# Eight chunks shared out anew: decay forms, router and norm forms, TensorE's order in chunk 1, and 72 increments ahead of VectorE's loop

## The chip, the core and the metric

One NeuronCore of a Trainium2 chip runs the whole program. The metric is its device time in microseconds, the median of three runs. All arithmetic that counts is float32.

## What is computed

The input is x, 8 sequences of 1024 tokens with 256 features. Four blocks follow one another, each with a normalization ahead of it and a residual sum behind it:

```python
x = x + scan_block(layernorm(x))      # selective scan, 512 channels x 16 states
x = x + ffn(layernorm(x))             # 16 experts, top 6, softmax gates
x = x + attention(layernorm(x))       # flow attention, linear in the tokens
x = x + ffn(layernorm(x))             # the same experts again
```

The scan block is what matters here:

```python
x_in, z = split(layernorm(x) @ in_proj)          # 256 -> 2 x 512
x_conv  = silu(conv4(x_in))
Bm, Cm  = split(x_conv @ x_proj)                 # 16 + 16
delta   = clip(softplus(x_conv @ dt_proj), 1e-4, 10)
h = exp(clip(delta * A, -10, 0)) * h + delta * Bm * x_conv   # token by token
h = h * min(1, 10 / |h|)                         # at every 16th token only
y = sum(Cm * h) + D * x_conv
out = layernorm(x + (y * silu(z)) @ out_proj)
```

The norm of h over its 16 states is looked at after every 16th token, so a scan runs over 16 tokens and no more before it must be bounded.

## The kernel before

**Tiles and chunks.** The 8192 tokens are 64 tiles of 128 tokens. Channels lie on partitions (4 blocks of 128), so a tile has 4 x 16 = 64 rows of states for each partition. A tile is worked through in eight chunks (c = 0 to 7) of 16 tokens. In each chunk GpSimd writes the inputs u * B into the state buffer (`inputs`, L394), ScalarE writes the decays into PSUM (`exponentials`, L456), VectorE runs one scan over 64 x 17 elements (`scan`, L1022), ScalarE squares the last states (`squares`, L462), VectorE sums them (`reduce`, L1030), ScalarE makes the factor (`norms`, L468 and L473), and VectorE bounds the states for the next chunk (`bound`, L1040 and L1043). GpSimd multiplies the states by C (`product`, L363), and TensorE transposes and sums these products in four quarters (`sum_states`, L730).

**Stages in step i.** Each engine has its own instruction list and an order written out by hand in its `step(i, k, stages)`; semaphores alone tie the engines together. Around the scan of tile i, a step also does the front of the tiles behind it (normalization of tile i + 4, projection and convolution of tile i + 3, gate and delta of tile i + 2), the back of tile i - 1 and i (return of the sums by `copy_sums` and `sums_back`, gating L1185, output projection L831, second norm L1194 to L1224, residual sum L414), the router of tile i - 2 (`route_norm`, `route`, `logits`, `route_scores`, `route_step`, `route_gate`), and the experts of tile i - 3 (`experts_mm` L764 on TensorE, one pair of experts a chunk; `expert_sums` L1106 on VectorE, two forms a chunk).

**Decay forms.** Ahead of the exponentials, ScalarE makes relu(10 + delta * A) for all 128 tokens of a tile, one activation for each of the 64 rows (`decays`, L447). They are those of tile i + 1, made during step i. `DECAYS` gives the first row of each chunk: chunks 0 to 7 make 6, 7, 6, 11, 7, 13, 14 and 0 of them. The first of a tile waits until delta is there, and the last releases the next tile's exponentials.

**VectorE's chunk.** `start(c)` is the scan and the two expert sums, `halfway(c)` the sum of squares, `end(c)` the bound; the forms of the other stages are placed between them. `route_step` has eight small steps for the choice of six experts; `router(lo, hi)` issues some of them. In chunk 3 both last norm forms (L1221, L1224) are made. `route_gate` makes the selection (L1096) and the gates (L1098) in chunk 7. GpSimd's `extra` makes u in chunk 1, sz (silu of z) in chunk 4, the gated xcv in chunk 5 and the residual sum in chunk 7.

**TensorE in chunk 1.** First the return of the sums (`sums_back`, L738, which waits for ScalarE's copy yT, L479), then the transposes of the router's input (`route`, L746), then the input projection (L823, which waits for xnT, L574).

**Loops.** `pipeline` unrolls the first and the last tiles. Between them every engine runs a loop of its own in which one turn is two tiles: on VectorE 28 turns from tile 4 on, on ScalarE 27 from tile 6 on. VectorE's increments at its start (`head_start`) and `settle` are instructions that only add to a semaphore.

After the 64 tiles the second stage (`merged`, some 1570 us) does attention and the second experts; in it VectorE calls `route_gate` once a tile.

## Time and profile before

| | us |
|---|---|
| median of 3 runs | 4571.68 |
| lowest, highest | 4569.64, 4571.75 |
| the profiled execution | 4568.96 |
| its span, first to last instruction | 4567.2 |
| TensorE busy | 4017.2 |
| VectorE busy | 3473.9 |
| ScalarE busy | 3079.6 |
| GpSimd busy | 2647.6 |

The profile is one execution on the chip. Engines are PE (TensorE, with PEld for its weight loads), DVE (VectorE), ACT (ScalarE), POOL (GpSimd) and SP (the queue that issues the transfers). A timeline row gives the start, the duration, the engine, the line of the kernel, what is written and read, a count where several are merged, and in brackets how long the engine was idle before it and what released it. The releaser is inferred; where the engine named had long been done, the cause is another one. Busy sums count overlaps of one instruction's end with the next one's start twice, so a full engine can seem slightly more than full.

### The profile page before, as it was taken

The page shows a single profiled execution, that of the slowest core. Times are in us where ns is not written, and L with a number is a line of the kernel's source. Part 1 is how long each engine was busy: PE and PEld are TensorE (multiplying, and loading weights), DVE is VectorE, ACT ScalarE, POOL GpSimd, SP SyncE. Part 2 cuts the span into 40 slices and gives each one's busy share as a digit, 9 for nine tenths or more (in the row PEclk, how much of TensorE's full clock was granted, in tenths as well). Part 3 has the DMA queues.
Part 4 walks back from the last instruction along what each step waited for, and adds up shares of the span by engine and source line. Part 5 has one row for each costly group of instructions (what it writes and reads, how often), then busy time and mean ns, then how long its engine had stood idle before and what let it go on. Part 6 is the DMA issues. An engine that isn't in the chain of part 4 may idle for free. (4 is left out here: it accounts for less than half of the span.)

```text
span 4567.2 us, 72130 instructions
## 1 busy us (share of the span) xinstructions
PE 4017.2 (88%) x19008; PEld 2604.4 (57%) x19008; DVE 3473.9 (76%) x7970; ACT 3079.6 (67%) x9040; POOL 2647.6 (58%) x1412
## 2 busy tenths in 40 slices
PE   6788888888888888888888888877999999999999
PEld 5666666566665666656666566643454454454454
DVE  4788888888888888888888888884566666676576
ACT  6888888888888888888888888863333333323321
POOL 5988988888888898888888888880000000000000
PEclk8999999999999999999999999999999999999999
DMA  3111111111111111111111111110000000000000
GB/s 112 52 58 52 59 49 49 57 53 55 51 49 57 49 62 49 49 57 49 56 55 49 57 49 51 59 48 15 23 16 8 16 16 6 16 17 6 6 8 10
DMA packets 91401, 188.71 MB, mean 41 GB/s; under 512 B 15872, under 2 KB 57600, under 8 KB 90624
## 3 DMA queue, kind: packets, MB, share of 16 engines
q1 hardware_dynamic: 91136, 186.11, 12.5%
q14 instruction: 213, 1.74, 0.1%
q8 instruction: 52, 0.85, 0.1%
HBM read 168.24 MB, written 17.83 MB: 41 GB/s over the span
## 5 line engine op out<-in xcount | busy, mean ns | idle before, releaser
L764 PE MATMUL ps<-w_x,mxT 128*128 128x512 f32 x4096 | 1994.7, 616 | 172.9 <-DVE macc L1106 171.5
L1106 DVE SCALAR_TENSOR_TENSOR macc<-ps,gate,macc 128x256 f32<-128x256 f32 x2048 | 981.0, 479 | 556.1 <-PE ps L764 458.5
L1022 DVE TENSOR_TENSOR_SCAN hb<-ps_dA,hb 128x1088 f32<-128x1088 f32 x512 | 1240.5, 2423 | 138.7 <-POOL hb L394 68.9
L394 POOL TENSOR_TENSOR hb<-u,bbc 128x1024 f32<-128x1024 f32 x512 | 1202.5, 2349 | 246.5 <-DVE hb L1040 199.5
L363 POOL TENSOR_TENSOR prod<-hb,cbc 128x1024 f32<-128x1024 f32 (+2 forms) x640 | 1190.0, 1864 | 136.0 <-DVE hb L1022 94.5
L764 PEld LDWEIGHTS ps<-w_x,mxT 128*128 128x128 f32 x4096 | 739.8, 195 | 894.3 <-issue 606.2
L447 ACT ACTIVATE zr<-dt,aneg 128x128 f32<-128x128 f32 x4096 | 1240.1, 388 | 0.0
L456 ACT ACTIVATE ps_dA<-zr 128x1024 f32<-128x1024 f32 x512 | 518.5, 1013 | 0.0
L730 PE MATMUL ps<-ident,prod 128*128 128x128 f32 x4096 | 493.8, 274 | 14.1 <-POOL prod L363 14.1
L730 PEld LDWEIGHTS ps<-ident,prod 128*128 128x128 f32 x4096 | 459.5, 142 | 19.7 <-POOL prod L363 17.6
L462 ACT ACTIVATE sq<-hb 128x64 f32<-128x64 f32 x512 | 158.1, 309 | 295.5 <-DVE hb L1022 292.1
L509 ACT ACTIVATE ex<-lgt,ms 128x16 f32<-128x16 f32 x128 | 39.2, 306 | 356.7 <-DVE ms L1063 356.5
L847 PEld LDWEIGHTS ps<-xin,dcw 128*128 128x128 f32 x2048 | 240.9, 193 | 21.3 <-issue 19.5
L877 PEld LDWEIGHTS ps<-xcv,w_dt 128*128 128x128 f32 x2048 | 245.3, 196 | 2.0
L877 PE MATMUL ps<-xcv,w_dt 128*128 128x128 f32 x2048 | 244.3, 279 | 0.0
L847 PE MATMUL ps<-xin,dcw 128*128 128x128 f32 x2048 | 240.9, 276 | 0.0
L823 PE MATMUL ps<-xnT,w_in 128*128 128x128 f32 x1024 | 185.4, 358 | 4.9 <-ACT xnT L574 3.5
L823 PEld LDWEIGHTS ps<-xnT,w_in 128*128 128x128 f32 x1024 | 179.5, 272 | 5.8 <-ACT xnT L574 4.0
L1040 DVE SCALAR_TENSOR_TENSOR hb<-ps_dA,hb 128x64 f32<-128x64 f32 x480 | 127.8, 266 | 67.9 <-ACT ps_dA L473 66.8
L738 PE MATMUL ps<-ident,yT 128*128 128x128 f32 x256 | 59.6, 320 | 135.4 <-ACT yT L479 135.4
L1030 DVE TENSOR_REDUCE nrs<-sq 128x4 f32<-128x64 f32 x512 | 110.2, 215 | 88.5 <-ACT sq L462 85.0
L738 PEld LDWEIGHTS ps<-ident,yT 128*128 128x128 f32 x256 | 33.5, 155 | 239.1 <-ACT yT L479 205.8
(200 smaller groups left out, 4850.5 us busy)
## 6 DMA issues: line engine op xcount, KB each, us to landing
bbc<-bcd SPq DMA_DIRECT2D x128, 512.0 KB, 3.7
cbc<-bcd SPq DMA_DIRECT2D x128, 512.0 KB, 3.7
xt<-in_x SPq DMA_DIRECT2D x128, 128.0 KB, 3.3
x2d<-macc SPq DMA_DIRECT2D x64, 128.0 KB, 1.7
out_dram<-macc SPq DMA_DIRECT2D x64, 128.0 KB, 1.7
w_x<-in_w_x SPq DMA_DIRECT2D x1, 4096.0 KB, 15.5
hb<-x2d SPq DMA_DIRECT2D x32, 128.0 KB, 2.3
sz<-x2d SPq DMA_DIRECT2D x16, 128.0 KB, 2.2
```

Of the source, the lines that this page charges most:

```text
L363: return TT(dst, states, cc, ALU.mult)
L394: TT(hb[c % 2][:].rearrange("p (e n) s -> p e n s", e=EB)[:, :, :, 1:SL], u[k][:, :, t0:t0 + CH].rearrange("p e (n s) -> p e n s", n=1).br ...
L447: last = act(zr[k][:, s, :], dt[:, s // N, :], ACT.Relu, bias=10.0, scale=aneg[:, s:s + 1])
L456: act(dA3[:, :, 1:SL], zr[k][:, :, c * CH:(c + 1) * CH], ACT.Exp, bias=-10.0).then_inc(M["dA"], 1)
L462: act(sq[:], hb[c % 2][:, :, CH:SL].rearrange("p a b -> p (a b)"), ACT.Square).then_inc(M["sq"], 1)
L730: last = mm(YT[:, h * P:(h + 1) * P], prod[:, n, h % 2 * QT:(h % 2 + 1) * QT, :].rearrange("p t e -> p (t e)"), ident[:], start=(h % 2 == ...
L764: last = mm(banks[p % len(banks)][:], mxT[k][:, j, :], w_x[:, j, p * 512:(p + 1) * 512], start=(j == 0), stop=(j == KD - 1))
L823: last = mm(F0[:, m * P:(m + 1) * P], w_in[:, j, m * P:(m + 1) * P], xnT[:, j, :], start=(j == 0), stop=(j == KD - 1))
L847: last = mm(F0[:, e * P:(e + 1) * P], dcw[:, e * TAPS + t, :], xin[:, e, t:t + P], start=False, stop=(e == EB - 1 and t == TAPS - 1))
L877: last = mm(F0[:, m * P:(m + 1) * P], w_dt[:, e, m * P:(m + 1) * P], xcv[k][:, e, :], start=False, stop=(m == EB - 1 and e == EB - 1))
L1022: V.tensor_tensor_scan(states, dA, states, 0.0, ALU.mult, ALU.add).then_inc(M["scan"], 1)
L1106: STT(macc[k][:], banks[(e // 2) % len(banks)][:, (e % 2) * D:(e % 2 + 1) * D], gate[k][:, e:e + 1], macc[k][:], ALU.mult, ALU.add).then_i ...
```

## The change

The decay forms per chunk become 5, 10, 5, 11, 6, 11, 11 for chunks 0 to 6, and the first 5 of the following tile are made in chunk 7, behind the delta that they need. GpSimd makes sz in chunk 3 instead of 4. TensorE does the input projection first in chunk 1, then the router's transposes, then the return of the sums. On VectorE the last norm form goes from chunk 3 to 4; the router's steps 2 and 3 go from chunk 5 to 4, steps 4 and 5 from chunk 6 to 5, and steps 6 and 7 stay in chunk 6, the first of them now ahead of the sum of squares' place; the selection becomes a helper of its own, `route_selection`, and goes from chunk 7 to 6 (in the second stage it stays where it was). Ahead of VectorE's loop stand 72 more increments of the settle semaphore. `DECAYS` now has eight entries: the chunk's first row for chunks 0 to 6, and the total. No instruction is added to or taken from a tile.

```diff
@@ -22,7 +22,7 @@
 X, TOPK = 16, 6
 ROUTER = 11
 DT_TOP, DT_BOTTOM = math.log(math.expm1(10.0)), math.log(math.expm1(1e-4))
-DECAYS = (0, 6, 13, 19, 30, 37, 50, 64, 64)
+DECAYS = (5, 10, 20, 25, 36, 42, 53, 64)
 
 
 AHEAD = 64
@@ -401,7 +401,7 @@
                     g.wait_ge(M["ldt"], AHEAD + i + 2)
                     g.wait_ge(M["xcv"], AHEAD + i + 2)
                     TT(u[1 - k][:], dt[:], xcv[1 - k][:], ALU.mult).then_inc(M["u"], 1)
-                if c == 4 and "G" in stages:
+                if c == 3 and "G" in stages:
                     g.wait_ge(M["ss"], AHEAD + i + 2)
                     g.wait_ge(M["yg"], AHEAD + (i if "B" in stages else 0))
                     TT(sz[1 - k][:], zt[:], sg[:], ALU.mult).then_inc(M["sz"], 1)
@@ -613,8 +613,10 @@
                             act(dt[:], dtt[:], ACT.Ln, bias=1.0).then_inc(M["ldt"], 1)
                         if X_ and in_time(i, X // 2 - 1):
                             route_init(i - 2, k, x1b[k][:], lambda: a.wait_ge(R["o"][k], AHEAD + (i - 2 - k) * 8))
-                    if G_ and DECAYS[c] < DECAYS[c + 1]:
+                    if G_ and c < NC - 1:
                         decays(i + 1, 1 - k, DECAYS[c], DECAYS[c + 1])
+                    if F and c == NC - 1:
+                        decays(i + 2, k, 0, DECAYS[0])
                     if c == 0 and B:
                         copy_sums(i - 1, 1)
                     if c == 5 and S_:
@@ -809,11 +811,6 @@
                     if c == 0 and B:
                         sum_states(i - 1, 3)
                     if c == 1:
-                        if B:
-                            sums_back(i - 1, 1)
-                        if X_:
-                            pe.wait_ge(M["bcv"], AHEAD + min_tiles(i + 2, stages))
-                            route(i - 2, k, F1)
                         if isinstance(i, int) and i == -2:
                             pe.wait_ge(s_win, 16)
                         if F:
@@ -823,6 +820,11 @@
                                     last = mm(F0[:, m * P:(m + 1) * P], w_in[:, j, m * P:(m + 1) * P],
                                               xnT[:, j, :], start=(j == 0), stop=(j == KD - 1))
                             last.then_inc(M["xi"], 1)
+                        if X_:
+                            pe.wait_ge(M["bcv"], AHEAD + min_tiles(i + 2, stages))
+                            route(i - 2, k, F1)
+                        if B:
+                            sums_back(i - 1, 1)
                     if c == 2:
                         if B:
                             pe.wait_ge(M["yg"], AHEAD + i)
@@ -1090,10 +1092,13 @@
                     v.wait_ge(R["router"], AHEAD + n * ROUTER + 8)
                     TS(ms[:, 12:13], ms[:, 5:6], ms[:, 8:9], 1e-10, ALU.mult, ALU.mult).then_inc(R["router"], 1)
 
-            def route_gate(n, k):
+            def route_selection(n):
 
                 v.wait_ge(R["router"], AHEAD + n * ROUTER + 5)
                 TT(selp[:], ex[:, 0:X], rest[:, 0:X], ALU.subtract).then_inc(R["router"], 1)
+
+            def route_gate(n, k):
+
                 v.wait_ge(R["router"], AHEAD + n * ROUTER + 10)
                 TS(gate[k][:], selp[:], ms[:, 9:10], None, ALU.mult).then_inc(R["router"], 1)
 
@@ -1219,14 +1224,15 @@
                     V.reciprocal(sc[:, 12:13], sc[:, 11:12]).then_inc(M["r3"], 1)
                     v.wait_ge(M["r3"], AHEAD + i)
                     STT(oo[:], oo[:], mv[:, 2, 0:1], ga_row[:], ALU.subtract, ALU.mult).then_inc(M["o3"], 1)
+                end(3)
+
+                start(4)
+                router(0, 2)
+                halfway(4)
                 if B:
                     v.wait_ge(M["o3"], AHEAD + i)
                     STT(oo[:], oo[:], sc[:, 12:13], be_row[:], ALU.mult, ALU.add).then_inc(M["o4"], 1)
-                end(3)
-
-                start(4)
-                router(0, 2)
-                halfway(4)
+                router(2, 4)
                 if G_:
                     v.wait_ge(M["r1"], AHEAD + i + 2)
                     V.tensor_copy(r1b[1 - k][:], r1a[1 - k][:]).then_inc(M["keep"], 1)
@@ -1236,9 +1242,9 @@
                 end(4)
 
                 start(5)
-                router(2, 3)
+                router(4, 5)
                 halfway(5)
-                router(3, 4)
+                router(5, 6)
                 if F:
                     v.wait_ge(M["z"], AHEAD + i + 3)
                     v.wait_ge(M["sz"], AHEAD + (i + 2 if G_ else 0))
@@ -1249,18 +1255,19 @@
                 end(5)
 
                 start(6)
-                router(4, 5)
                 if L_:
                     v.wait_ge(M["st1"], AHEAD + i + 4)
                     settle()
                     V.bn_aggr(mv[:, 0, :], st[:, 0, :]).then_inc(M["mv1"], 1)
-                router(5, 6)
+                router(6, 7)
                 if L_:
                     v.wait_ge(M["mv1"], AHEAD + i + 4)
                     TS(sc[:, 0:1], mv[:, 0, 1:2], 1e-5, None, ALU.add).then_inc(M["vp"], 1)
                     TS(sc[:, 1:2], mv[:, 0, 1:2], D / (D - 1.0), 1e-30, ALU.mult, ALU.max).then_inc(M["vp"], 1)
                 halfway(6)
-                router(6, 8)
+                router(7, 8)
+                if X_:
+                    route_selection(i - 2)
                 end(6)
                 if L_:
                     v.wait_ge(M["qs"], AHEAD + i + 4)
@@ -1301,6 +1308,8 @@
             TT(left[96:P, :], left[96:P, :], rows_of_split[96:P, :], ALU.subtract).then_inc(s_split, 1)
             v.wait_ge(s_split, 4)
             V.tensor_copy(rows_of_split[96:P, :], left[96:P, :]).then_inc(s_zero, 1)
+            for _ in range(72):
+                settle()
             v.wait_ge(s_zero, 4)
             pipeline(v, step)
 
@@ -1420,6 +1429,7 @@
                         for q in range(4 * (p - 6), 4 * (p - 5)):
                             route_step(r + NTILES, q)
                     if p == 7:
+                        route_selection(r + NTILES)
                         route_gate(r + NTILES, r % 2)
                 if b < NB and not early:
                     attend(b, s)
```

## Rows read from the trace of the kernel before

**Rows 1.** Page, part 1: busy us (share) and instructions of each engine

```profile
PE 4017.2 (88%) x19008; PEld 2604.4 (57%) x19008; DVE 3473.9 (76%) x7970; ACT 3079.6 (67%) x9040; POOL 2647.6 (58%) x1412
```

**Rows 2.** Stretches: length, busy of PE, PEld, DVE, ACT, POOL, clock, DMA

```profile
190.68:2993.24 2802.56, 2393.64 (x13690) 1744.97 (x13688) 2354.01 (x4715) 2399.55 (x7256) 2440.90 (x1298) 0.95 0.16 53
```

**Rows 3.** Waits of VectorE, 190.68 to 2993.24: total us, times, longest

```profile
DVE hb L1022 <- POOL hb L394: 68.9, 21, 3.6
DVE macc L1106 <- PE ps L764: 67.9, 53, 2.0
DVE nrs L1030 <- ACT sq L462: 65.6, 176, 0.5
DVE hb L1040 <- ACT ps_dA L473: 54.8, 117, 0.7
DVE oo L1194 <- PE ps L831: 39.8, 59, 0.7
DVE hb L1022 <- issue: 18.6, 6, 3.1
```

**Rows 4.** Timeline of VectorE at a jump: start, us, line, operands [idle before]

```profile
1566.45 0.26 DVE L1043 SCALAR_TENSOR_TENSOR hb<-ps_dA,hb 128x64 f32<-128x64 f32 x1
1570.32 2.42 DVE L1022 TENSOR_TENSOR_SCAN hb<-ps_dA,hb 128x1088 f32<-128x1088 f32 x1 [3.61 <-POOL hb L394]
```

**Rows 5.** DMA queue 14: 1570.32:1663.14, then 1 us from 1568, 1571, 1584, 1616, 1651

```profile
q14 instruction: 5, 0.04, 0.2%
q14 instruction: 1, 0.01, 1.9%
q14 instruction: 1, 0.01, 2.0%
q14 instruction: 1, 0.01, 6.0%
q14 instruction: 1, 0.01, 5.2%
q14 instruction: 1, 0.01, 2.1%
```

**Rows 6.** Timeline of ScalarE at its jump

```profile
1566.70 0.49 ACT L505 ACTIVATE macc<-x1b,ms 128x256 f32<-128x256 f32 x1
1567.10 0.58 ACT L552 ACTIVATE xn<-xt,sc 128x256 f32<-128x256 f32 x1
```

**Rows 7.** Timeline of VectorE at the start

```profile
6.01 0.06 DVE L996 MEMSET c_eps<- 128x1 f32 x1 [6.01 <-issue]
```

**Rows 8.** Timeline of TensorE in tile 31, and at 1579

```profile
1521.56 0.44 PE L807 MATMUL ps<-ident,xn 128*128 128x128 f32 x2 [1.11 <-ACT xn L552]
1523.76 1.98 PE L764 MATMUL ps<-w_x,mxT 128*128 128x512 f32 x4
1528.37 0.44 PE L738 MATMUL ps<-ident,yT 128*128 128x128 f32 x2 [2.62 <-ACT yT L479]
1529.15 2.97 PE L823 MATMUL ps<-xnT,w_in 128*128 128x128 f32 x16
...
1579.13 1.95 PE L823 MATMUL ps<-xnT,w_in 128*128 128x128 f32 x16
```

**Rows 9.** Timeline of ScalarE, the projection's operand

```profile
1525.51 0.79 ACT L574 ACTIVATE xnT<-ps,be_in,ga_in 128x128 f32<-128x128 f32 x2
```

**Rows 10.** Stretch with the granted clock (0.50)

```profile
1530.00:1532.00 2.00, 2.00 (x11) 2.00 (x11) 1.64 (x3) 1.97 (x9) 2.00 (x3) 0.50 0.00 0
```

**Rows 11.** Timeline of ScalarE, decay forms and the square behind xn

```profile
1507.75 3.89 ACT L447 ACTIVATE zr<-dt,aneg 128x128 f32<-128x128 f32 x13
...
1522.84 0.31 ACT L462 ACTIVATE sq<-hb 128x64 f32<-128x64 f32 x1 [1.33 <-DVE hb L1022]
```

**Rows 12.** Timeline of VectorE, the bound of chunk 6

```profile
1513.39 0.27 DVE L1040 SCALAR_TENSOR_TENSOR hb<-ps_dA,hb 128x64 f32<-128x64 f32 x1 [0.71 <-ACT ps_dA L473]
```

**Rows 13.** Timeline of GpSimd, chunk 3

```profile
1544.20 2.35 POOL L394 TENSOR_TENSOR hb<-u,bbc 128x1024 f32<-128x1024 f32 x1 [1.29 <-DVE hb L1040]
```

6 lines of the change are left out of this document (3 added, 3 removed).

## Prediction

> **What bounds the kernel now.** I read the page first. VectorE, ScalarE, GpSimd and TensorE are all close to full until about 3000 us, then only TensorE is [rows 1]. The change touches the first stage (the scan over 64 tiles of 128 tokens); of the second it only splits one VectorE helper in two without moving an instruction, so I leave it alone. In the middle of the first stage, from the first scan of tile 3 to that of tile 62, 59 tiles take 2802.56 us, 47.5 us a tile [rows 2]. Divided by 59, the busy sums are 41.4 us for GpSimd, 40.7 for ScalarE, 40.6 for TensorE and 39.9 for VectorE: nothing is saturated, the tile is 6 us longer than its fullest engine. Where those microseconds are stands in VectorE's waits, since VectorE carries the serial chain (scan, square sum, bound, next scan) [rows 3]. The reader should see two kinds there.
>
> First, 27 waits before a scan, 68.9 + 18.6 = 87.5 us, 3.2 us each. They are one per turn of the loop (28 turns of two tiles, 27 jumps back). The one at 1570.32 starts when the last instruction of the turn, of 1566.45, is done, and nothing that it could wait for is late [rows 4]: the profile names a GpSimd instruction only because that is the last one before it.
>
> Second, waits for other engines inside the tile: 67.9 (expert sums for TensorE) + 65.6 (square sums for ScalarE) + 54.8 (bound for ScalarE) + 39.8 (residual for the output projection) = 228.1 us, 3.87 us a tile. Without both kinds a tile is (2802.56 - 87.5 - 228.1) / 59 = 42.15 us; that is VectorE's own work with its gaps.
>
> **Part 1: 72 increments ahead of VectorE's loop.** What are the 3.2 us? In the turn that starts at 1570, five packets of instructions are fetched, 0.04 MB, so 8 KB or 128 instructions of 64 bytes each [rows 5]. One lands in the gap itself, one right behind it, then one at 1584, 1616 and 1651. I counted in the instruction lists that the kernel builds to: VectorE has 526 instructions ahead of the loop and 339 in it, ScalarE 986 and 321. At 1584 VectorE stands at about number 50 of the loop, at 1616 (just in the second tile) at 176, at 1651 at 305: 128 apart. So blocks of 128 begin at numbers 50, 178 and 306, the loop lies in four of them, and with the next one fetched ahead the first has been dropped when the loop jumps back. ScalarE's loop of 321 shows what happens when it fits: at its jump, between the instruction at 1566.70 and the one at 1567.10, there is no gap [rows 6], and the five packets are all VectorE's. Three blocks and the one fetched ahead stay; that is my reading of two loops, an inference. If number 50 starts a block, the loop starts 78 into one; 72 more instructions move that to 150 - 128 = 22, and 22 + 339 = 361 is under 384: three blocks. ScalarE gets about 5 more instructions ahead of its loop; its absence of fetches says that it starts at most 63 into a block. So all 27 stalls go: **-87.5 us**. Bounds: 0 (the size of the store is not what I infer) and -87.5. I take the end, since a loop that fits is there to see.
>
> The Trainium skill, page "Runtime: NRT & Kernel Launch", section "Instruction fetch mechanics", speaks against this: it has 32 KiB of instructions in blocks of 16 KiB, only two lines, and a taken branch to a target outside that window stalls. By that rule 339 instructions never stay at any place, and this term would be 0. Packets of 8 KB and ScalarE's loop without a gap [rows 5, 6] disagree with it.
>
> The price of the increments is paid once, at 17 us, where VectorE goes straight from its set-up to the first instruction of the pipeline, on which the first convolution waits. VectorE's first 56 increments lie in the 6.01 us ahead of its first instruction [rows 7], so one costs at most 0.11 us: 72 cost 0 to 7.7. I take **+4**, since that row has the start of the program in it as well.
>
> **Part 2: TensorE's order in chunk 1.** Now TensorE holds at the return of the sums for ScalarE's copy of yT, 2.62 us at 1528.37, and the input projection behind it starts only at 1529.15, although its operand was done at 1526.30 [rows 9]. It then runs at half speed: 2.97 us against 1.95 in the next tile [rows 8], with a granted clock of 0.50, so 1.2 GHz [rows 10], after an idle of 2.6 us. The expert product behind it is late, and VectorE waits for it 53 times, 1.3 us each [rows 3]. With the projection first, TensorE works through that idle; the product and the output projection end some 2 us earlier. The waits of 67.9 and 39.8 go. What is late next: the sums return behind projection and transposes. The pair of 1523.76 is done at 1525.7; with part 3 that is 1527.2, plus 1.95 is 1529.15, plus some 0.6 for the two small steps is 1529.75, against 1528.8 now. VectorE's gating waits for it: about 0.4 us a tile is given back, part of it hidden by a wait of 0.2 that chunk 1 has now.
>
> **Part 3: decay forms.** 64 a tile as before, 0.30 us each (13 in 3.89 us) [rows 11]. Chunks 0 to 6 had 6, 7, 6, 11, 7, 13, 14 and get 5, 10, 5, 11, 6, 11, 11; chunk 7 had none and gets 5. ScalarE's sum is the same. The forms go away where ScalarE is late: the 176 waits for a square are three in a tile, 0.37 us each, in chunks 1, 5 and 7 [rows 3], and behind the 13 forms of chunk 5 the bound of chunk 6 waits 0.71 [rows 12]. With 2 and 3 forms fewer in chunks 5 and 6, 0.6 and 0.9 us, those go; chunk 0's loss of one takes 0.3 off the wait in chunk 1. What the five in chunk 7 cost: the normalized input xn of the next tile comes 1.5 us later. Now ScalarE has 1.33 us free behind it [rows 11], so the next square is late by about 0.2, in the shadow of two expert sums and the norm forms. TensorE stands idle for xn some 0.7 us longer than now (1.11 us [rows 8]), since the pair ahead of it ends later too in a tile without the other waits, and runs from there without a break.
>
> **Part 4: VectorE's forms and sz.** The last norm form goes from chunk 3 to 4, where two router forms join it; the selection goes from chunk 7 to 6. Chunks 4 and 6 grow, chunks 3, 5 and 7 shrink by as much together. Net 0: the count is the same, these chunks are VectorE's own either way, and what waits for them is off the path (the residual sum is in chunk 7; the convolution's result is needed by ScalarE only when its forms are done). GpSimd's sz goes from chunk 4 to 3, where GpSimd now waits 1.29 us for VectorE [rows 13], about the length of sz, and what follows in chunk 4 moves up by as much.
>
> **Sum.** Of 228.1 us of waits I leave 0.9 us a tile: 0.4 from part 2 and 0.5 for four engines that are then 93 to 96% full and meet with little to spare. That is 53 us left, **-175 us**; a tile is 43.05. Bounds: nothing left, -228, and half left, -114. Profiled execution: 4568.96 - 87.5 - 175 + 4 = 4310.5; its time is 2.7 below the median, so **4313 us**. With the bounds: 4260 to 4378.
>
> **The rivals.**
> (a) The clock falls elsewhere. TensorE idles nearly 2 us ahead of xn; idles of 1.3 us are not followed by a fall now, one of 2.6 is. If it falls there, the transposes, an expert pair and the projection (6 us of work) take up to 3 us more, and half of it comes back to VectorE through the returned sums: 1 to 1.5 us a tile, 59 to 89 us: 4372 to 4402. For it: that is exactly where the forms put the gap. Against: behind it TensorE is busy for 12 us on end. 16%.
> (b) The jump still costs 3.2 us, because the first block is dropped wherever the loop lies (or ScalarE's loop now loses its own): 4313 + 87 = 4400. For it: no loop of VectorE is to be seen without the gap. Against: [rows 5, 6]. 12%. This is the case that the rule of the Trainium skill, quoted above, gives.
> (c) Everything fits and nothing of the waits is left but 0.3 us a tile: 4270 to 4285. 10%.
> (d) Slower: the clock does not come back. If TensorE stays at 1.2 GHz for most of a tile, its 40.6 us of work grow: 12 us of full-speed work at half speed make 53, longer than the 47.5 of now, and TensorE bounds the tile; from 7 us on the gain is gone. For 59 tiles 5 us more is +300: about 4870. Against: granted clock is 0.95 over the stretch [rows 2], and every fall now ends within 4 us. 3%.
> (e) The moves gain only what they cost (an engine that is nearly full takes over) and the jump stays: within 0.2% of now. 2%.
>
> **How the numbers follow.** Forecast 57%, with its own range 4285 to 4360. The range must reach to (a) and (b): 4265 to 4402. A difference under 0.2% (9 us) can't be told from none here. Faster: forecast, (a), (b), (c) = 95%; same 2%, slower 3%.
>
> **What would show it.** No gap of 3 us before a scan, and no instruction packets in the middle of the stage: part 1 right. Input projection at 1.95 us in every tile and no wait of the expert sums in chunk 2: part 2. No wait of the bound in chunk 6: part 3. A granted clock under 1 in the first 10 us of a tile: (a). A tile above 44 us with no such stretch would mean that my shares of waits were not where the next limit is, which would make the prediction wrong.

## The result and the profile after

The changed kernel takes 4430.3 us (median of 4 runs, 4425.88 to 4433.15) against 4571.7 for the kernel before in the same session: a ratio of 0.9687, 95% interval 0.9671 to 0.9704. That is 141 us faster, and 117 us slower than the 4313 predicted, above the top of the range (4402). Its profiled execution has a span of 4427.8 us.

The table shows where the 139.4 us between the two spans lie (us, each stretch up to the next), counted from the first scan of tile 0, of tile 3 and of tile 62:

| stretch | before | after | difference | predicted |
|---|---|---|---|---|
| to the first scan | 62.20 | 70.05 | +7.85 | +4 |
| tiles 0 to 2 | 128.48 | 126.97 | -1.5 | 0 |
| tiles 3 to 61 | 2802.56 | 2656.93 | -145.6 | -262.5 |
| the rest | 1573.96 | 1573.85 | -0.1 | 0 |

All but some 2 us of the miss are in the middle of the first stage: 116.9 us. The busy sums of this stretch stand in the following row of the after kernel's stretches, to be read beside [rows 2] (columns: length, busy PE, PEld, DVE, ACT, POOL, granted clock, DMA share, GB/s). A tile takes 2656.93 / 59 = 45.03 us.

```profile
197.02:2853.95 2656.93, 2308.05 (x13692) 1702.80 (x13690) 2496.47 (x4715) 2391.34 (x7254) 2446.97 (x1299) 0.99 0.17 56
```

The reader should look at the third busy sum. VectorE has the same 4715 instructions as in [rows 2] and is busy for 142.5 us more. This sum is the stretch less the engine's idle time, so overlaps do not count twice in it, other than the text on the profile above has it; added up one by one, the durations of its instructions grew from 2531 to 2733 us. ScalarE and GpSimd are within 9 us of their sums there, and TensorE has 86 us less, its clock having risen from 0.95 to 0.99. The waits come first. These are VectorE's in the after kernel, same stretch (total us, times, longest), beside [rows 3]:

```profile
DVE sg L1190 <- PE ps L740: 36.3, 58, 1.2
DVE macc L1111 <- PE ps L766: 12.8, 12, 1.2
...
DVE nrs L1032 <- ACT sq L462: 3.7, 23, 0.2
```

No wait before a scan is left. Of the four kinds of 228.1 us, 16.5 are left (12.8 + 3.7), and a new kind has come, the gating's wait for the returned sums, 36.3. Together that is 52.8 us, 0.90 us a tile, just the sum that the prediction left standing. That it fits so well is partly luck: the gating has 0.6 where 0.4 was said, the others 0.3 where 0.5 was said. Still, the waits went as forecast. What went wrong is the rest of the tile: (2656.93 - 52.8) / 59 = 44.14 us, where the prediction had 42.15.

The groups of VectorE's instructions show where (a form is one instruction of an engine). Mean ns of one stands behind the busy sum. First four groups of the kernel before, from 200 to 2800 us, then the same four of after:

```profile
L1221 DVE SCALAR_TENSOR_TENSOR oo<-oo,mv,ga_row 128x256 f32<-128x256 f32 x55 | 26.7, 485 | 2.0
L1224 DVE SCALAR_TENSOR_TENSOR oo<-oo,sc,be_row 128x256 f32<-128x256 f32 x55 | 26.7, 485 | 2.0
L1096 DVE TENSOR_TENSOR selp<-ex,rest 128x16 f32<-128x16 f32 x54 | 31.6, 584 | 0.0
L1098 DVE TENSOR_SCALAR gate<-selp,ms 128x16 f32<-128x16 f32 x54 | 35.3, 654 | 1.9
```

```profile
L1226 DVE SCALAR_TENSOR_TENSOR oo<-oo,mv,ga_row 128x256 f32<-128x256 f32 x58 | 68.6, 1183 | 2.1
L1234 DVE SCALAR_TENSOR_TENSOR oo<-oo,sc,be_row 128x256 f32<-128x256 f32 x58 | 120.9, 2085 | 0.0
L1098 DVE TENSOR_TENSOR selp<-ex,rest 128x16 f32<-128x16 f32 x57 | 100.8, 1768 | 0.0
L1103 DVE TENSOR_SCALAR gate<-selp,ms 128x16 f32<-128x16 f32 x57 | 47.6, 836 | 0.0
```

The same instructions on the same operands: the last norm form takes 2085 ns instead of 485, the selection 1768 instead of 584, the first norm form 1183 instead of 485. Together the four have 5.87 us a tile instead of 2.21: 3.66 us, 216 us over the 59 tiles. No other group of VectorE changed by more than 3.0 us in the stretch, and those that changed by over 0.8 became shorter, some 14 us in all. The timeline of the after kernel, GpSimd and VectorE side by side, says what they wait for inside:

```profile
1432.27 2.24 POOL L363 TENSOR_TENSOR prod<-hb,cbc 128x1024 f32<-128x1024 f32 x1
1433.80 0.98 DVE L1226 SCALAR_TENSOR_TENSOR oo<-oo,mv,ga_row 128x256 f32<-128x256 f32 x1
1434.47 1.46 POOL L407 TENSOR_TENSOR sz<-zt,sg 128x512 f32<-128x512 f32 x1
...
1438.17 2.50 POOL L363 TENSOR_TENSOR prod<-hb,cbc 128x64 f32<-128x64 f32 x2
1438.77 2.18 DVE L1234 SCALAR_TENSOR_TENSOR oo<-oo,sc,be_row 128x256 f32<-128x256 f32 x1
...
1450.35 2.27 POOL L363 TENSOR_TENSOR prod<-hb,cbc 128x1024 f32<-128x1024 f32 x1
1450.87 1.78 DVE L1098 TENSOR_TENSOR selp<-ex,rest 128x16 f32<-128x16 f32 x1
```

Each form starts under a GpSimd product and ends when it does: the last norm form at 1440.95, the product at 1440.67; the selection at 1452.65, the product at 1452.62. The first norm form starts at 1433.80, the product ends at 1434.51, and the form ends 0.27 us behind it. It is so in all 59 tiles of the stretch: each of the four forms starts under a GpSimd instruction and ends just behind it, the norm forms by 0.26 to 0.28 us (but for two of the first, which end behind the next one), the selection and the gate by 0.02 to 0.04. The selection and the gate already were held so in all 59 tiles of the kernel before, for a shorter remainder. There, the two norm forms ran in the hole of 1.29 us that [rows 13] shows on GpSimd:

```profile
1540.66 2.25 POOL L363 TENSOR_TENSOR prod<-hb,cbc 128x1024 f32<-128x1024 f32 x1
1542.85 0.48 DVE L1221 SCALAR_TENSOR_TENSOR oo<-oo,mv,ga_row 128x256 f32<-128x256 f32 x1
1543.37 0.48 DVE L1224 SCALAR_TENSOR_TENSOR oo<-oo,sc,be_row 128x256 f32<-128x256 f32 x1
```

The product ends at 1542.91 and the next GpSimd instruction starts at 1544.20; but for the first 0.06 us both forms lie between. The four long groups have their inputs and their output in SBUF. Forms of VectorE that read PSUM (xin, zt, the gating) kept their 0.68 to 0.69 us, xin at 1433.01 under the first of these products.

**What the theory is, and its rival.** Theory: those four forms are held by GpSimd's instructions, which costs the 2 us a tile that the prediction lacks. Rival: the held time costs nothing by itself, since VectorE would wait anyway, and the missing 2 us come from TensorE, whose idle time ahead of the normalized input grew from the 1.11 us of [rows 8] to 2.4 to 2.5, with the clock falling behind it in some tiles. For the theory speaks that 47 of the 59 tiles show no fall of the clock and still take 44.7 us.

### The profile page after: what moved, and what is told of

It is laid out like the page before. It is cut to its first block, busy times and chain, and to the rows that moved or that the text cites. A ratio compares the mean times of both kernels' runs of the same rounds, so it can differ in the third digit from the quotient of the medians.

```text
span 4427.8 us, 72202 instructions
## 1 busy us (share of the span) xinstructions
PE 3935.4 (89%) x19008; PEld 2565.6 (58%) x19008; DVE 3621.2 (82%) x7970; ACT 3072.6 (69%) x9040; POOL 2654.1 (60%) x1412
## 4 chain that ended last, share of the span: by engine, by line
PE 49%; issue 22%; DVE 15%; POOL 5%; ACT 4%; DVEq 1%; ACTq 0%; POOLq 0%
PE ps L766 27%; DVE macc L1111 6%; PE ps L879 5%; POOL prod L363 3%; PE ps L914 3%; PE ps L732 2%; PE ps L820 2%; PE ps L896 2%; ACT zr L447 2%; POOL xcv L410 2%; PE ps L872 1%; PE ps_dA L914 1%; DVE xin L1221 1%; DVE sg L1286 1%; DVE xcv L1241 1%
## 5 line engine op out<-in xcount | busy, mean ns | idle before, releaser
L766 PE MATMUL ps<-w_x,mxT 128*128 128x512 f32 x4096 | 1967.9, 609 | 202.1 <-DVE macc L1111 202.1
L766 PEld LDWEIGHTS ps<-w_x,mxT 128*128 128x128 f32 x4096 | 730.0, 192 | 932.5 <-issue 599.4
L363 POOL TENSOR_TENSOR prod<-hb,cbc 128x1024 f32<-128x1024 f32 (+2 forms) x640 | 1191.2, 1866 | 53.0 <-DVE hb L1024 44.8
L732 PE MATMUL ps<-ident,prod 128*128 128x128 f32 x4096 | 507.7, 279 | 14.6 <-POOL prod L363 14.6
L809 PE MATMUL ps<-ident,xn 128*128 128x128 f32 x128 | 28.7, 307 | 166.5 <-ACT xn L552 164.2
L820 PEld LDWEIGHTS ps<-xnT,w_in 128*128 128x128 f32 x1024 | 128.8, 198 | 34.0 <-issue 16.6
L809 PEld LDWEIGHTS ps<-ident,xn 128*128 128x128 f32 x128 | 13.1, 143 | 216.0 <-ACT xn L552 110.2
L861 PEld LDWEIGHTS ps<-xnT,w_in 128*128 128x128 f32 x1024 | 124.4, 192 | 21.3 <-issue 19.5
L914 PE MATMUL ps<-zr,prod 128*128 128x512 f32 x288 | 134.4, 592 | 0.0
L820 PE MATMUL ps<-xnT,w_in 128*128 128x128 f32 x1024 | 130.1, 282 | 4.1 <-ACT xnT L574 4.1
```

The costliest lines, as they stand in the source:

```text
L363: return TT(dst, states, cc, ALU.mult)
L732: last = mm(YT[:, h * P:(h + 1) * P], prod[:, n, h % 2 * QT:(h % 2 + 1) * QT, :].rearrange("p t e -> p (t e)"), ident[:], start=(h % 2 == ...
L766: last = mm(banks[p % len(banks)][:], mxT[k][:, j, :], w_x[:, j, p * 512:(p + 1) * 512], start=(j == 0), stop=(j == KD - 1))
L820: last = mm(F0[:, m * P:(m + 1) * P], w_in[:, j, m * P:(m + 1) * P], xnT[:, j, :], start=(j == 0), stop=(j == KD - 1))
L914: last = mm(QUAD[s % 4][:], w_a[:, w, kk, j * P:(j + 1) * P], xTa[:, kk, g * TG:(g + 1) * TG], start=(kk == 0), stop=(kk == KD - 1))
```

## The experiments

All ratios are against runs of the kernel before on the same chip; after is 4430.3 us. Those with one run only have no ratio. The runs belong to five sessions, in which the kernel before had medians of 4563.9 to 4573.4 us, so a difference from after of 15 us or less isn't clear of noise by the times alone; where it matters, the middle stretch of the profiled executions stands beside it (after: 2656.93 us).

### 1. The increments alone, and the change without them

Kernel before with nothing but the 72 increments:

```diff
             v.tensor_copy(rows_of_split[96:P, :], left[96:P, :]).then_inc(s_zero, 1)
+            for _ in range(72):
+                settle()
             v.wait_ge(s_zero, 4)
```

> The kernel before with nothing but the 72 increments ahead of VectorE's loop. Theory (the loop fits into three blocks of 128 instructions and is kept): the 27 waits of 87.5 us go, the start costs the 6.3 us seen in the changed kernel, so about 4490, with 79 instruction packets instead of 213 and in-tile waits as before (3.9 us a tile). Rival (the gap is hidden in the changed kernel by something else that changed, place decides nothing): 213 packets, the 27 gaps stay, about 4578.

Measured: 4476.8 us, ratio 0.9795 (0.9776 to 0.9814). The waits of 87.5 us are gone and the others are as they were in [rows 3], 3.83 us a tile; the tile went from 47.50 to 45.91, and the first scan moved from 62.20 to 68.67. Instruction packets, from the page's DMA part: 213 in the kernel before, here

```profile
q14 instruction: 78, 0.64, 0.0%
```

The other way round, the changed kernel without the increments:

> The changed kernel without the 72 increments; all moved forms stay. Theory: the gap of 3.2 us is back at each of 27 jumps and the start is 6.3 us shorter: 4430 + 87.5 - 6.3 = 4511, 213 packets. Rival (the gap came from the old order of the forms): no gap, about 4424.

Measured: 4514.9 us, ratio 0.9876 (0.9856 to 0.9896), 214 packets, and the gap is back at each jump:

```profile
1547.72 2.42 DVE L1024 TENSOR_TENSOR_SCAN hb<-ps_dA,hb 128x1088 f32<-128x1088 f32 x1 [3.31 <-POOL hb L394]
```

And the changed kernel with 100 increments in place of 72, so that the loop starts 50 into a block of 128 (22 + 28) and 50 + 339 = 389 is over 384:

> The changed kernel with 100 increments ahead of VectorE's loop instead of 72. Theory (blocks of 128, four kept, the loop starts 78 + 100 - 128 = 50 into one and 50 + 339 = 389 is over 384): the loop lies in four blocks again, the 27 gaps and some 213 packets are back: 4430 + 87.5 + 2.5 = 4520. Rival (any shift that moves the loop far enough is good): no gap, 79 packets, 4433.

Measured: 4569.4 us (one run), 213 packets, and in the stretch from 200 to 2800 us:

```profile
DVE hb L1024 <- POOL hb L394: 74.6, 21, 4.1
...
DVE hb L1024 <- issue: 14.8, 5, 3.2
```

The gap is back at 26 jumps, all that lie in that stretch. So it isn't the presence of increments, but where the loop begins: by the prediction's count starts of 22, 50 and 78 into a block were tried, and only 22, with the loop in three blocks, is without the gap. The total is 49 us above what was expected. A further 0.33 us stands ahead of xin once a turn (8.9 in all), where the profile names nothing that it waits for, and 27 of 59 tiles have the long chunk 1 described in 6, against 12 in after.

### 2. Three forms back in their old places

The changed kernel with the last norm form in chunk 3, the selection in chunk 7 and sz in chunk 4:

```diff
-                if c == 3 and "G" in stages:
+                if c == 4 and "G" in stages:
...
                     STT(oo[:], oo[:], mv[:, 2, 0:1], ga_row[:], ALU.subtract, ALU.mult).then_inc(M["o3"], 1)
+                if B:
+                    v.wait_ge(M["o3"], AHEAD + i)
+                    STT(oo[:], oo[:], sc[:, 12:13], be_row[:], ALU.mult, ALU.add).then_inc(M["o4"], 1)
...
-                if X_:
-                    route_selection(i - 2)
...
                 if X_:
+                    route_selection(i - 2)
                     route_gate(i - 2, k)
```

> The changed kernel with three moves undone: the last norm form back in chunk 3, sz back in chunk 4, the selection back in chunk 7. Theory (VectorE's forms that take both operands from SBUF are held while a GpSimd form runs, and the three moves put them into GpSimd's busy times): last norm form from 2.09 to about 0.49 us, the one before it from 1.17 to 0.49, selection from 1.77 to 0.59, together 3.5 us a tile less VectorE time; part of it comes back as waits, so a tile of 42 to 43.3 instead of 45.03 and 4250 to 4330 in all. Rival (the tile is held by another engine, and VectorE's longer forms only fill the time): the forms are short again but waits take their place, tile 44.5 to 45, 4410 to 4430.

Measured: 4388.6 us, ratio 0.9605 (0.9587 to 0.9623): 42 us faster than after, and above the range expected. The forms are short again, the selection at 909 ns and the last norm form, by its group (200 to 2800 us), at 485:

```profile
L1229 DVE SCALAR_TENSOR_TENSOR oo<-oo,sc,be_row 128x256 f32<-128x256 f32 x59 | 28.6, 485 | 2.1
```

But the waits are not those of after. From 200 to 2800 us of this kernel:

```profile
DVE macc L1111 <- PE ps L766: 43.3, 81, 0.7
DVE sg L1190 <- PE ps L740: 42.9, 58, 1.2
DVE hb L1042 <- ACT ps_dA L473: 37.9, 58, 0.7
DVE nrs L1032 <- ACT sq L462: 14.0, 84, 0.2
```

138 us now stand there where after has 52.5. The tile without its waits is 41.96 us, the floor of the prediction (42.15) or a little less. So the theory holds for the floor, and the rival is right on the larger part of the sum: the tile without its waits lost 2.18 us against after, and the waits took 1.48 of it back. Not all of that comes from the short forms. In chunk 7, sz in chunk 4 delays ScalarE's silu of xcv by 0.41 us, and the expert product behind it is late by 0.66, some 40 us in all. With the selection back and sz left in chunk 3 (experiment 4) VectorE waits only 12.5 us for it there, so some 27 us are the price of moving sz. In chunk 6, without the selection, VectorE arrives at the bound 0.66 us before ScalarE's factor.

### 3. One operand from PSUM

To see whether it is the operand and nothing else, the last norm form stays in chunk 4 and reads its second operand from a PSUM bank, which holds the convolution's result, in place of the bias row in SBUF. It leaves out the norm's bias in all tiles but the last ones.

```diff
-                    STT(oo[:], oo[:], sc[:, 12:13], be_row[:], ALU.mult, ALU.add).then_inc(M["o4"], 1)
+                    if F:
+                        v.wait_ge(M["conv"], AHEAD + i + 3)
+                        STT(oo[:], oo[:], sc[:, 12:13], F0[:, 0:D], ALU.mult, ALU.add).then_inc(M["o4"], 1)
+                    else:
+                        STT(oo[:], oo[:], sc[:, 12:13], be_row[:], ALU.mult, ALU.add).then_inc(M["o4"], 1)
```

> The changed kernel, with the last norm form at the same place in chunk 4 but its second operand read from a PSUM bank (the convolution's, free at that time) instead of the bias row in SBUF. That leaves out the addition of the norm's bias row in all tiles but the last ones. Theory (two operands in SBUF are what is held): the form takes about 0.49 us instead of 2.09, all else as before it, and the tile loses up to 1.6 us. Rival (the form is held by its place, for example its input or its output is awaited): still about 2.1 us.

Measured (one run): 4391.1 us. The group and the timeline of this kernel:

```profile
L1236 DVE SCALAR_TENSOR_TENSOR oo<-oo,sc,ps 128x256 f32<-128x256 f32 x59 | 27.8, 471 | 0.0
```

```profile
1419.37 2.49 POOL L363 TENSOR_TENSOR prod<-hb,cbc 128x64 f32<-128x64 f32 x2 [0.20 <-DVE hb L1024]
1420.45 0.47 DVE L1236 SCALAR_TENSOR_TENSOR oo<-oo,sc,ps 128x256 f32<-128x256 f32 x1
```

Same place, same size, same product beside it: 471 ns instead of 2085, and in all 59 tiles it ends 0.79 us or more before the product does. That is the holding, shown. Of the 1.61 us of this form, 95 us over 59 tiles, 39 reached the time; the neighbours took some (first norm form 1362 instead of 1183, selection 1899 instead of 1768), and waits for TensorE rose from 49.1 to 89.0 (52.6 for the gating, 36.4 for the experts). The 36 waits for the experts stand in chunk 1, and just as many tiles of this kernel have the long chunk 1 of experiment 6.

### 4. One form at a time

The selection alone back in chunk 7:

> The changed kernel with the selection back in chunk 7, next to the gates. Theory (held by GpSimd's product in chunk 6): 1.77 us becomes 0.6 to 0.9, chunk 6 shrinks by 1.1 at most and chunk 7 grows by 0.6, so 0.3 to 0.6 us a tile, 4395 to 4412. Rival: the wait for the bound's factor in chunk 6 takes its place in full, 4430.

Measured: 4415.2 us, ratio 0.9666 (0.9643 to 0.9689), 15 us less than after and just outside what was expected; the two ratios' intervals overlap, but the middle stretch is 12.9 us shorter as well (2644.05). The selection takes 917 ns, the gate 655: 1.03 us less a tile held, with the first norm form 1.18 in all. 20.5 us of it came back as the bound's wait for ScalarE's factor in chunk 6.

The last norm form alone back in chunk 3, sz staying there too:

> The changed kernel with the last norm form back in chunk 3, sz staying there too. Theory: GpSimd is busy there now, with the product and then sz, so the form is held until sz is done, 1.2 to 1.7 us instead of 2.09: chunk 4 loses 2.1, chunk 3 gains 1.2 to 1.7; a gain of 0.4 to 0.9 us a tile, 4380 to 4408. Rival (the form is short wherever the convolution's neighbourhood is left): 0.49 us, 4340.

Measured: 4388.9 us, ratio 0.961 (0.9587 to 0.9632), as expected. It takes 1258 ns here, not 485, since sz now fills the hole of [rows 13]. This kernel is as fast as that of experiment 2, although its four forms have 5.15 us a tile and those have 2.82: how long the forms are held does not by itself tell the time.

Both together, with the increments moved out of the start into VectorE's part of step -2:

> The changed kernel with the last norm form back in chunk 3 and the selection back in chunk 7, sz still in chunk 3, and the increments inside VectorE's first step. Theory: the gains of the two runs before add up (41 and 15 us against the changed kernel's 4430), and the start's 6.3 us come on top: 4360 to 4375. Rival: they overlap, 4385.

Measured: 4383.9 us, ratio 0.9601 (0.9585 to 0.9618): only 5 us better than the norm form alone, where the first scan alone comes 6.8 us earlier (63.94 against 70.76). The gains of the two forms don't add. From 200 to 2800 us of this kernel, the bound's wait for ScalarE's factor is back with 26.4 us, and the gating's wait is 43.6 where after has 36.0.

### 5. TensorE's order back

The changed kernel with the old order in chunk 1 (return of the sums, router's transposes, projection):

> The changed kernel with TensorE's old order in chunk 1 (return of the sums, transposes, then the input projection). Theory (the new order is what ends VectorE's wait in chunk 2): chunk 2 grows by the 1.5 to 2 us that it lost, chunk 1 gives back about 0.5, so 1 to 1.5 us a tile, 4490 to 4520. Rival (the decay forms alone would have done it): within 15 us of 4430.

Measured: 4436.5 us, ratio 0.9714 (0.9698 to 0.973). The rival named there was right and the expectation wrong by 54 us: the new order is worth 6 us, both in the times and in the middle stretch (2662.89), and the ratios' intervals just overlap. Waits from 200 to 2800 us:

```profile
DVE macc L1111 <- PE ps L766: 32.4, 31, 1.2
DVE oo L1199 <- PE ps L833: 25.0, 57, 0.8
```

The waits for the output projection (39.8 in [rows 3]) and for the experts (67.9) are there as the old order makes them, but smaller, a bound's wait of 6.2 stands beside them, and the gating's 36.3 is gone. The sum is 1.13 us a tile against 0.90: the new order exchanges one set of waits for another.

### 6. TensorE's idle time ahead of the normalized input, and the clock

In after, 12 of the 59 tiles take about 46.3 us instead of 44.7, with 6.6 to 6.9 us in chunk 1 where the others have 5.1 to 5.2. TensorE's timeline at the start of such a tile, and then of a normal one:

```profile
1505.94 0.43 PE L809 MATMUL ps<-ident,xn 128*128 128x128 f32 x2 [2.50 <-ACT xn L552]
1506.21 2.89 PE L732 MATMUL ps<-ident,prod 128*128 128x128 f32 x16
1508.90 2.62 PE L766 MATMUL ps<-w_x,mxT 128*128 128x512 f32 x4
```

```profile
1461.15 0.44 PE L809 MATMUL ps<-ident,xn 128*128 128x128 f32 x2 [2.42 <-ACT xn L552]
1461.42 1.91 PE L732 MATMUL ps<-ident,prod 128*128 128x128 f32 x16
1463.17 1.88 PE L766 MATMUL ps<-w_x,mxT 128*128 128x512 f32 x4
```

After an idle of 2.50 us the transposes take 2.89 instead of 1.91 us and an expert pair 2.62 instead of 1.88. The granted clock stands in the last column but two, first for 2 us of the slow tile and then for 8 us of the normal one:

```profile
1508.00:1510.00 2.00, 2.00 (x8) 1.48 (x7) 1.87 (x2) 1.91 (x8) 1.78 (x2) 0.50 0.03 7
1461.00:1469.00 8.00, 7.85 (x48) 5.85 (x49) 6.84 (x15) 7.56 (x26) 7.78 (x5) 1.00 0.28 79
```

0.50 is 1.2 GHz, 1.00 is 2.4 GHz. To take the idle time away, the five forms in chunk 7 go:

```diff
-DECAYS = (5, 10, 20, 25, 36, 42, 53, 64)
+DECAYS = (0, 5, 15, 23, 34, 42, 53, 64)
...
-                    if F and c == NC - 1:
-                        decays(i + 2, k, 0, DECAYS[0])
```

> The changed kernel with no decay forms in chunk 7: chunks 0 to 6 make 5, 10, 8, 11, 8, 11, 11. Theory (the five forms hold back xn by 1.5 us, TensorE idles 2.4 us ahead of it, the clock falls in about one tile of five and the sums' return is 0.5 us late in the others): idle back to 1.1 us or less, no tile of 46.3, the wait of the gating for the sums gone, so 0.5 us off most tiles and 1.9 off eleven, 4380 to 4400. Rival (ScalarE is full and the forms cost as much in chunks 2 and 4): 4430 or more.

Measured: 4415.8 us, ratio 0.9673 (0.965 to 0.9697). TensorE's idle ahead of xn fell from 140.0 to 57.8 us between 200 and 2800 us (1.0 us a tile), no tile has the long chunk 1, and the granted clock is 1.00 over the whole middle: the clock part is as expected. The gain is 15 us, not 30 or more, and the ratios' intervals overlap; the middle is 12.2 us shorter (2644.76). Two waits stand, 200 to 2800 us:

```profile
DVE nrs L1030 <- ACT sq L462: 37.0, 86, 0.6
DVE sg L1188 <- PE ps L738: 27.9, 57, 0.5
```

The forms that left chunk 7 delay the square of chunk 3 (32.9 us), and the return of the sums still stands behind projection and transposes.

### 7. The forms together, and the best kernel

All four forms back to back at the end of chunk 6, increments in step -2, `DECAYS` (5, 10, 20, 25, 34, 40, 50, 64):

> The changed kernel with all four forms that GpSimd holds (both norm forms, selection, gates) one behind another at the end of chunk 6, the 72 increments inside VectorE's first step where it waits for TensorE anyway (two times 36), and decay forms 5, 10, 5, 9, 6, 10, 14, 5. Theory (a form is held until the running GpSimd form ends; behind it the next ones slip in while VectorE has the port): one hold a tile instead of four, so the four forms take 2.5 to 3 us together instead of 5.87; start 6 us shorter; a tile of 42.8 to 43.8 and 4290 to 4355 in all. Rival (each form is held anew, since GpSimd takes its turn between two): some 5 us again, 4400 to 4430.

Measured: 4379.9 us, ratio 0.9592 (0.9576 to 0.9608), above the range expected. Of the 50 us that it gains on after, 7.6 lie ahead of the first scan, since the increments now stand where VectorE waits anyway; the middle gains 41, as much as in experiment 2. Two tiles of this kernel:

```profile
1422.96 0.47 DVE L1269 SCALAR_TENSOR_TENSOR oo<-oo,mv,ga_row 128x256 f32<-128x256 f32 x1
1423.07 2.58 POOL L363 TENSOR_TENSOR prod<-hb,cbc 128x1024 f32<-128x1024 f32 x1
1423.35 0.17 DVE L1098 TENSOR_TENSOR selp<-ex,rest 128x16 f32<-128x16 f32 x1
1423.47 2.45 DVE L1274 SCALAR_TENSOR_TENSOR oo<-oo,sc,be_row 128x256 f32<-128x256 f32 x1
1425.84 0.22 DVE L1103 TENSOR_SCALAR gate<-selp,ms 128x16 f32<-128x16 f32 x1
...
1465.98 1.24 DVE L1269 SCALAR_TENSOR_TENSOR oo<-oo,mv,ga_row 128x256 f32<-128x256 f32 x1
1466.87 2.46 POOL L363 TENSOR_TENSOR prod<-hb,cbc 128x1024 f32<-128x1024 f32 x1
1467.14 2.22 DVE L1098 TENSOR_TENSOR selp<-ex,rest 128x16 f32<-128x16 f32 x1
1469.28 0.47 DVE L1274 SCALAR_TENSOR_TENSOR oo<-oo,sc,be_row 128x256 f32<-128x256 f32 x1
```

Free, the four take 0.47, 0.17, 0.47 and 0.22 us. In a group, not all of them pay: in 36 of the 59 tiles one is held and the others pass, in 23 two are, the first norm form and the selection. In the second tile shown, the first norm form ends at 1467.22, behind the GpSimd instruction ahead of the product, which ends at 1466.93, and the selection at 1469.36, behind the product, which ends at 1469.33. Which ones they are changes from tile to tile. The four have 3.69 us a tile instead of 5.87. But 36 of 59 tiles now have the long chunk 1 with the clock fall, and the waits are 2.06 us a tile. The last experiment takes that away as in 6:

```diff
-DECAYS = (5, 10, 20, 25, 34, 40, 50, 64)
+DECAYS = (0, 5, 15, 23, 32, 40, 50, 64)
```

> The same kernel as the grouped one (the four norm and router forms together at the end of chunk 6, the increments inside VectorE's turn, 4379.9 us), with one thing changed: no decay form in chunk 7; the 64 are 5, 10, 8, 9, 8, 10, 14 in chunks 0 to 6. In the grouped kernel 59.4 us of waits stand ahead of the expert sums and 56.0 ahead of the gating, and both were in the tiles whose clock is low in the first 10 us. Theory (the clock falls because TensorE stands idle some 2.5 us for the normalized input, which chunk 7's forms hold back): no tile with chunk 1 over 6 us, expert-sum waits down from 59.4 to 10 to 20, gating waits from 56 to about 30, TensorE's products back from 291 to 270 to 277 ns; against that 0.6 us in every second tile for a square, some 18 us: 4325 to 4350 us. Rival (the sums' return and the square take the gain, as in the kernel without the five forms that kept its own place for the norm forms, where only 15 us were left): 4360 to 4375. Rival 2 (the clock falls anyhow): 4380 or more.

Measured: 4356.8 us (4352.78 to 4357.07), ratio 0.9544 (0.9528 to 0.956), between the two ranges given, 3 us from the rival's. No tile has a long chunk 1 (only tile 3 still has the clock fall, behind an idle of 2.1 us), the transposes of the products are at 273 ns a piece against 291, and no wait of VectorE for the experts is left. What came instead is the square, more than the 18 us allowed for it:

```profile
DVE nrs L1032 <- ACT sq L462: 50.0, 145, 0.6
DVE sg L1190 <- PE ps L740: 27.8, 57, 0.5
```

The clock fall is not gone altogether. In 11 of the 59 tiles it now comes in chunk 6, behind an idle of 1.9 us for GpSimd's gated xcv; the second row is the stretch just behind, with the granted clock at 0.53:

```profile
1364.99 1.06 PE L872 MATMUL ps<-xcv,w_xp 128*32 128x128 f32 x8 [1.90 <-POOL xcv L410]
1366.00:1369.00 3.00, 3.00 (x16) 2.97 (x16) 3.00 (x7) 2.94 (x13) 3.00 (x2) 0.53 0.00 0
```

It is the fastest kernel here, 4.6% under before. Against after it is 73 us less as the times stand and 65 by the ratios; 65 lie in the middle stretch (2591.64) and 7.5 ahead of the first scan.

### All of them in one table

Per tile, first scan of tile 3 to that of tile 62, in us. Waits are VectorE's for other engines and those for which the profile names nothing; "rest" is the tile less these and less the gap at the jump; "held" is the sum of the four forms' mean times; the last column counts the tiles with over 5.7 us in chunk 1. It does not count every fall of the clock: with TensorE's order back the granted clock is at 0.50 for over 1 us in 32 tiles, and in the kernel before in 56, mostly in chunks 1 and 2.

| kernel | tile | waits | jump | rest | held | slow tiles |
|---|---|---|---|---|---|---|
| before | 47.50 | 3.88 | 1.48 | 42.13 | 2.21 | 0 |
| 72 increments only | 45.91 | 3.83 | 0 | 42.08 | 2.21 | 0 |
| after | 45.03 | 0.90 | 0 | 44.13 | 5.87 | 12 |
| after without increments | 46.61 | 1.01 | 1.52 | 44.09 | 5.67 | 15 |
| after with 100 increments | 47.29 | 1.74 | 1.59 | 43.96 | 5.66 | 27 |
| TensorE's order back | 45.13 | 1.13 | 0 | 44.00 | 5.59 | 1 |
| none in chunk 7 | 44.83 | 1.11 | 0 | 43.71 | 5.46 | 0 |
| selection back | 44.81 | 1.31 | 0 | 43.51 | 4.69 | 12 |
| last norm form back | 44.37 | 0.76 | 0 | 43.60 | 5.15 | 8 |
| operand in PSUM | 44.36 | 1.54 | 0 | 42.82 | 4.57 | 36 |
| two forms back | 44.35 | 1.60 | 0 | 42.75 | 3.78 | 24 |
| three forms back | 44.34 | 2.38 | 0 | 41.96 | 2.82 | 23 |
| grouped | 44.34 | 2.06 | 0 | 42.28 | 3.69 | 36 |
| grouped, none in chunk 7 | 43.93 | 1.50 | 0 | 42.42 | 3.75 | 0 |

Roughly the rest follows the held time: between the increments alone and after it grew by 2.05 us for 3.66 us held, 0.56 for each. Of the other 1.61 us a tile, 0.24 is that other instructions of VectorE became shorter. About 0.95 is that the records of neighbours overlap more: the durations grew by 3.43 us a tile and VectorE's busy time by 2.47. Some 0.42 fell into pauses that VectorE had anyway, too short for the list of waits. And the waits rise as the rest falls: no kernel here has both the 42.1 of the one and the 0.9 of the other, which is what the prediction added up. Yet the waits of the kernels with a short rest have different causes (sz in chunk 4, the clock fall in 36 tiles, the square behind the forms that left chunk 7), so no run shows that the two can't be had together.

## Why the prediction was wrong, step by step

**Part 1, the increments: right.** -87.5 us in the middle, measured -93.7 alone (2802.56 to 2708.82 for the 59 tiles), some 6 us more than the gaps themselves. The starts of 22, 50 and 78 all did what three blocks of 128 and one fetched ahead say. The price at the start was 6.3 us, not 4: VectorE's first xin stands behind an idle of 6.33 us, 0.088 us for each increment. That is inside the bounds (0 to 7.7); the first scan came 7.85 later, 1.7 of it from other edits, since without the increments it is at 63.87 against 62.20. Rival (b) is out. The rule of the Trainium skill that was quoted for it, page "Runtime: NRT & Kernel Launch", section "Instruction fetch mechanics" (two blocks of 16 KiB), does not describe this case: the packets are 8 KB (0.64 MB in 78), and whether the loop stays turns on its lying in three or four blocks of 128 instructions.

**Part 2, TensorE's order: the effect was right, the size not its own.** The waits of 67.9 and 39.8 us went to 12.8 and 0, and the gating waits 0.6 us a tile where 0.4 was said. But experiment 5 shows that with the other edits in place the order is worth 6 us. With the old order 58.5 of the 107.7 us still stand (33.1 + 25.4), so nearly half went with the other edits; the new order takes 45.7 of these away and puts 36.3 ahead of the gating in their place. That the longer tile of VectorE gives TensorE time to catch up is a likely reason for the first half, but no run shows it by itself.

**Part 3, the decay forms: right, with one term too small.** The square's wait fell from 65.6 to 3.7 us and the bound's from 54.8 to 0. TensorE's idle ahead of xn was to grow by 0.7 us; it grew by 1.3 to 1.4, from 1.11 to 2.42 to 2.50. Rival (a) was to be 59 to 89 us with a fall in every tile. It came in 12 tiles of 59, 1.6 us each: 19 us. In experiment 6, where it is gone, the middle is 12 us shorter, with other waits in its place.

**Part 4, the forms of VectorE: here it failed.** The sentence was "Net 0: the count is the same, these chunks are VectorE's own either way". It took for granted that an instruction costs the same wherever it stands. The last norm form went from a hole in GpSimd's work under a product; sz went into the very hole of [rows 13] in which both norm forms had run; the selection went under the product of chunk 6. The row was read as "GpSimd is free here" and not as "who uses it that GpSimd is free here". The price is 3.66 us a tile in the records and 2.0 in the tile without its waits: 2.0 x 59 = 118 us, the size of the miss. It isn't what undoing the moves gives back: experiment 2 has the short rest again and gains 42 us only, as other waits come out.

The prediction's own last sign came true, too: "A tile above 44 us with no such stretch". 47 of the 59 tiles take 44.3 to 44.8 us without the clock fall.

The Trainium skill, page "SBUF — State Buffer", section "SBUF: two separate sides", has the rule that was missed: VectorE and GpSimd share a port pair as an exclusive lock held for a whole instruction; a VectorE operation needs it with two SBUF inputs (against a GpSimd operation that reads SBUF) or in a performance mode that uses two ports, whichever starts first has it, and "the other fully blocks". The trace agrees: the last norm form is held until the product's end to within 0.3 us in all 59 tiles, and free again with one input in PSUM (471 ns against 2085). GpSimd is busy for 92% of the stretch, so outside its pauses each such form was to be charged up to a product's 2.25 us, an estimate from the rows above.

**The sum: the waits right, the addition wrong.** 53 us of waits were left standing and 52.8 were found. The floor of 42.15 us is real too, it returns at 41.96 in experiment 2. In these kernels they don't come together: each one with a short rest has 1.5 to 2.4 us of waits. The held forms cost time and, as it seems, gave ScalarE and TensorE room. So the forecast of 43.05 us a tile lacked two things, the holding (+2.0 in the kernel as built) and, had the forms been short, another 0.6 to 1.5 of waits. Had only the last been missing, the time would have been about what experiment 2 gives, 4389, within the range of 4265 to 4402 and still 76 above the forecast. The best kernel, at 43.93, still lies 0.9 above. (The bounds of the sum, 4260 and 4378, aren't worked out alike: with the +4 of the lower one the upper is 4374. Nothing hangs on it.)

**What stays open.** Why an idle of 2.4 to 2.5 us ahead of xn is followed by the clock's fall in 12 tiles of one kernel and in 36 of another with the same idle sum (140.0 and 142.5 us) isn't settled. Kernels with 1.9 to 2.0 us there have it in 12 to 24 tiles; behind 1.0 to 1.1 us it was not seen. Reading the selection's or the first norm form's operands from PSUM wasn't tried, so the full price of the holding with nothing else moved isn't measured. Nor was a kernel made with short forms, no clock fall and no late square at once.

## What to carry to other kernels

Before a VectorE instruction with all operands in SBUF is moved, look in the timeline at what GpSimd does at the old and at the new place; give it a place where GpSimd waits, give it an operand in PSUM, or put such instructions side by side so that not all of them pay. A hole in one engine's row can be what makes another's instruction short, so filling it isn't free. And a floor measured while there are waits, and waits measured on top of a longer floor, must not be added up as if they were independent.

## What the runs showed of the chip that was not expected

- A form of VectorE of 0.47 us with both inputs in SBUF takes up to 2.45 us under a GpSimd product, which itself took 2.58 there instead of 2.25; a selection of 128 x 16, 0.17 us when free, takes 2.22. The form with one SBUF input and a scalar (the gate, 0.22 free) is held as well: 0.65 on average in before and 0.83 in after, in all 59 tiles until 0.03 us behind the end of GpSimd's instruction.
- Held instructions are no idle time: VectorE's busy sum rose by 142.5 us with the same number of instructions, and the list of waits shows nothing of it.
- A loop of 339 instructions pays 2.8 to 4.1 us at each jump (3.2 to 3.5 on the mean of a kernel) when it starts 50 or 78 into a block of 128 instructions, by the count above, and nothing when it starts 22 into one. An increment that only adds to a semaphore costs 0.088 us on VectorE.
- Which instruction of a group is held can change from tile to tile: in the grouped kernel it is the last norm form in one and the first norm form and the selection in another, with chunk 6 at 7.7 or 8.4 us.
